# A bound on the indices of every gather in a relational graph network on one core

## What is computed

```
for l in range(n_layers):                       # 3 layers
    xr  = jnp.einsum('nd,rde->rne', x, W_rel[l])   # 8 types
    msg = xr[edge_type, src]
    agg = jax.ops.segment_sum(msg, dst, num_segments=x.shape[0])
    x   = jax.nn.relu(agg + x @ W_root[l] + bias[l])
```

## Time and profile before

| what | value |
|---|---|
| three runs, median | 5964.4 us |
| three runs, lowest and highest | 5960.87 and 5973.35 us |
| the profiled execution: its span, from first to last instruction | 5964.9 us |
| gathers on POOL | 4633, 947 ns each, 4389.2 us |
| matmuls with the gathered rows (L421) | 18792, 2700.1 us |
| matmuls with the relation matrices (L492) | 5568, 1273.8 us |
| bytes moved | 674.77 MB, mean 113 GB/s |

### The profile page before, as it was taken

The page is one execution under the profiler, slowest core; times in us unless marked ns, Lnnn a source line. Parts: engine busy times, 40 slices in busy tenths (PEclk is TensorE's granted clock), DMA queues, the critical chain, the costliest instruction groups (busy, mean ns, idle before and its releaser), DMA issues.

```text
span 5964.9 us, 107654 instructions
## 1 busy us (share of the span) xinstructions
PE 4310.7 (72%) x26040; PEld 3901.4 (65%) x26041; DVE 1844.7 (31%) x3589; ACT 619.0 (10%) x848; POOL 4396.5 (74%) x4659
## 2 busy tenths in 40 slices
PE   4777777777777767777777777766776777776776
PEld 3666666666676656666666666666676666666666
DVE  5222222222222222222222222223333334333333
ACT  3001010010101000000000001000101011101111
POOL 5777777777777677777777777767777777777774
PEclk8898989898989888889999999888888888888887
DMA  6333333333333333333333333333333333333332
GB/s 196 113 111 113 112 112 112 111 114 111 113 112 112 107 111 110 111 111 111 110 111 111 111 110 112 110 106 113 114 113 115 113 113 114 114 113 114 113 113 74
DMA packets 296167, 674.77 MB, mean 113 GB/s; under 512 B 86202, under 2 KB 147387, under 8 KB 295772
## 3 DMA queue, kind: packets, MB, share of 16 engines
q0 software_dynamic: 222384, 607.55, 35.2%
q1 hardware_dynamic: 44686, 37.38, 2.1%
q10 hardware_dynamic: 28702, 26.46, 1.3%
HBM read 645.38 MB, written 25.68 MB: 112 GB/s over the span
## 4 chain that ended last, share of the span: by engine, by line
PE 27%; POOL 25%; issue 20%; SPq 15%; DMA 6%; DVEq 3%; DVE 3%; ACT 1%; ACTq 0%
POOL rows L403 25%; PE bank L421 15%; SPq L352 13%; PE bank L492 10%; DMA rows<-node_table,idx 5%; SPq L347 3%; DVE agg L1003 1%; ACT agg L708 1%; DVEq L986 1%; DVEq L989 1%; PE bank L618 1%; DVEq L1093 1%; PE bank L611 0%; DVE onehot L908 0%; PE bank L537 0%
## 5 line engine op out<-in xcount | busy, mean ns | idle before, releaser
L403 POOL DMA_INDIRECT rows<-node_table,idx x4633 | 4389.2, 947 | 1504.1 <-issue 1316.2
L421 PE MATMUL bank<-onehot,rows 128*128 128x128 f32 x18792 | 2700.1, 305 | 1422.5 <-DVE agg L1003 705.8
L421 PEld LDWEIGHTS bank<-onehot,rows 128*128 128x128 f32 x18792 | 2564.0, 218 | 1571.8 <-issue 1553.2
L1003 DVE TENSOR_TENSOR agg<-bank,agg 128x256 f32 x1566 | 663.7, 424 | 2079.8 <-PE bank L421 1575.6
L492 PE MATMUL bank<-wrel,agg 128*128 128x256 f32 x5568 | 1273.8, 388 | 44.4 <-DVE agg L1016 34.2
L492 PEld LDWEIGHTS bank<-wrel,agg 128*128 128x128 f32 x5568 | 1073.4, 195 | 200.0 <-issue 53.9
L908 DVE TENSOR_TENSOR onehot<-bank,key 128x1152 f32<-128x1152 f32 x525 | 707.0, 1347 | 0.0
L708 ACT COPY agg<-zero_col 128x2304 f32 x174 | 367.2, 2111 | 2928.9 <-PE bank L492 2928.9
L1025 DVE SCALAR_TENSOR_TENSOR acc<-bank,in_first,acc 128x256 f32 x174 | 84.2, 484 | 1777.6 <-PE bank L492 1680.9
L611 PE MATMUL bank<-wroot,nextT 128*128 128x256 f32 x392 | 146.7, 510 | 0.0
L715 ACT COPY acc<-bank 128x256 f32 (+1 forms) x98 | 36.5, 372 | 1004.7 <-PE bank L611 1004.7
(11 more groups left out here) (138 smaller groups left out, 800.1 us busy)
## 6 DMA issues: line engine op xcount, KB each, us to landing
far_rows<-node_table SPq DMA_DIRECT2D x7168, 1.0 KB
rows<-node_table,idx POOLq DMA_INDIRECT x4633
node_table<-new_x ACTq DMA_DIRECT2D x98, 128.0 KB
x_tile<-node_table SPq DMA_DIRECT2D x58, 128.0 KB, 2.2
x_in<-in_x_dram SPq DMA_DIRECT2D x8, 768.0 KB, 11.2
wrel<-in_L_gnn_W_rel_dram SPq DMA_DIRECT2D x6, 1024.0 KB, 8.2
xres<-in_x_dram ACTq DMA_DIRECT2D x48, 128.0 KB
out_dram<-res ACTq DMA_DIRECT2D x48, 128.0 KB
```

The source lines that it names most:

```text
L403: pool.indirect_dma_start(rows[:, s:s + D], None, tables[layer % 2], bass.IndirectOffsetOnAxis(ap=idx[:, g * TPG + k, j:j + 1], axis=0),). ...
L421: last = nc.tensor.matmul(to[:, h, :], of[:, s:s + P], hot[:, hot_k * CH + j, :], start=(j == 0), stop=(j == CH - 1))
L1003: nc.vector.tensor_tensor(window, seg[k % 3].rearrange("p h (r w) -> p h r w", r=R), window, ALU.add).then_inc(agg_added, 1)
```

## The change

Every gather of L403 is given a bound, NP_ - 1 = 6271, the last row of the table, and `oob_is_err=False`: an index above the bound would be skipped silently, its row not written. Before, no bound was given, and `oob_is_err` was at its default, true. The arguments apart, the kernel's text is the same, and the gathers, their order, their sources and destinations, their semaphores and the number of them are the same.

In the program that is built the bound is not part of the instruction but stands in a register. Each gather names a register, and ahead of each of the 4633 gathers POOL's stream has one instruction more that moves the number 6271 into it. Where a gather carried a wait for `seg_ready` (or for `stored`), that wait is now on the move ahead of it, and the gather has none.

```
                             pool.indirect_dma_start(
                                 rows[:, s:s + D], None, tables[layer % 2],
-                                bass.IndirectOffsetOnAxis(ap=idx[:, g * TPG + k, j:j + 1], axis=0),
+                                bass.IndirectOffsetOnAxis(ap=idx[:, g * TPG + k, j:j + 1], axis=0), bounds_check=NP_ - 1, oob_is_err=False,
                             ).then_inc(gathered[k], 16)
```

## The result

The changed kernel took 6193.1 us (median of 4 runs, 6191.28 to 6198.0), the kernel before 5968.9 us in the same comparison. The ratio is 1.0378, with a 95% interval of 1.0363 to 1.0392: 224 us slower. The forecast of no change, 5965 us, was wrong; the range of 5940 to 6480 us and the larger chance of slower held.

A forecast was written before the change was run, and what follows sets the result against it. POOL's gather cadence was taken to bound the kernel: 5964.9 us before, + 0 for the move, under 1.1 for the wait, 0 for the check, gave 5965 us; the 8-in-10 range was 5940 to 6480 us.

The forecast's parts named there:

- What bounds the kernel: POOL's gathers, one every 1.25 us, set the time; anything added to one gather is paid 4633 times.
- The three true stops: POOL's real waits before gathers: one of 6.4 us at the start and two layer changes of 51.8 us together.
- The register move: One move ahead of each gather in POOL's stream, hidden by the sequencer's run-ahead: 0, at most 162 us.
- The sign that I named: In POOL's queue, 4633 MOVE of about 35 ns inside the gathers' bodies would show that the step held.
- The wait on the move: PE's wait, shifted to the move ahead of the gather, costs only at three stops: under 1.1 us, taken as 0.
- The check of 128 indices: Inside each gather, comparing its indices with the bound: taken as 0, between ends of -507 and +990 us.
- The comparison per row: Rival: a new step per row in the gather's body, 107 ns a gather, 6460 us for one step; chance 0.22.
- The small fixed price: Rival: reading the bound or choosing a branch once per gather, 14 to 162 us, 6034 us at 15 ns; chance 0.17.
- The move that is not hidden: Rival: the gap between gathers grows from 305 by 35 ns, bodies unchanged, 6127 us; chance 0.13.
- the cheaper silent mode: Rival: no out-of-range reporting at each gather's end saves, say, 10 ns a gather, 46 us, giving 5919 us; chance 0.13.
- the bound is ignored: Rival: the descriptor code doesn't use the bound, 5965 us, within the forecast; no separate chance given.
- The tail: From the end of POOL's last gather to the execution's end: 56.1 us in the sum of the kernel before.

The follow-up runs named there:

- e9: The changed kernel itself, no edit, timed beside the kernel before and the one-move kernel: 6206.0 us, ratio 1.0385 to the kernel before.
- e10: The changed kernel with its bound register loaded once ahead of all gathers and the waits back on the gathers: 6207.1 us, ratio 1.0381 to the kernel before.
- e3: The changed kernel with oob_is_err=True, an index over the bound being an error: 8459.1 us, ratio 0.9968 to the kernel before, which took about 8480 us there.
- e7: The kernel before with gathers of 64 rows in place of 128, no bound: 8553 us in one execution, median gather body 903 ns.
- e8: Gathers of 64 rows as in e7, with a bound in a register loaded once: 8491 us in one execution, median gather body 942 ns.
- e4: The kernel with one move for all gathers, its bound lowered to 3124 so about half the rows are skipped: body 998 ns, no time given.

## Why the prediction was right and wrong, step by step

*What bounds the kernel* was right. POOL's cadence sets the time, a nanosecond a gather is 4.6 us, and the sum over POOL (bodies, gaps, head, tail) closes in the changed kernel too. The three true stops leave out a fourth, 35.3 us for the first table, which lies inside the 50.8 us of the head, so the sum stands.

*The register move* was priced right, at 0 (e9 against e10), and for the right reason: POOL's sequencer works ahead under gathers too, by about twelve of them. The sign that I named was the wrong one: most moves lie not inside the bodies but just behind a gather's end, and they are those of later gathers. They took 29 ns, not 35. At the start of layer 0, 19 of them had run when 8 gathers had started.

*The wait on the move* was taken at under 1.1 us, with a move and a decode at each of three stops. It cost 0.52 us at each, about 1.6 us, which the times can't show. Where a wait had to be sat out, the gather started 0.78 us after the release with the wait on the move, and 0.26 us after it with the wait on the gather. With POOL starved it is more, as forecast: e3, with the wait on the move, has 591 stops, by the estimate above up to 307 us.

*The check of 128 indices* is the step that failed: "I take 0", from the argument that a loop must compare with some bound anyway. It is 52 ns, and 4633 x 52 = 241 us, the 245 of the bodies. The argument stood on no row, and it was put over the nearest row. The ends that I kept, -507 and +990 us, held it. That the range of 5940 to 6480 us held too is owed to its width and not to a price: its upper end came from a CAST, whose slope the gathers don't follow.

*The rivals.* The comparison per row had the right place and sign (body longer, gap the same). Its 107 ns, from the slope of a CAST, 0.835 ns an element, are twice the whole price and four times the 26 ns of it that go by rows by the straight line. By the same line a row of the gather itself costs 0.67 ns, so the 7.4 ns a row that I read from 947 / 128, my support for a loop of nine steps, was mostly a fixed cost of 860 ns spread over rows; what POOL does in that time, which I took for the making of descriptors row by row, no run opens. The small fixed price had its share too, 26 ns. By this estimate the two rivals together make what happened. That neither does alone is what e7 and e8 show, with 39 ns at 64 rows. The move that is not hidden fell, at e10 and by the moves that run ahead; the cheaper silent mode fell against no bound, though it is cheaper than the error mode. That the bound is ignored fell at e4.

*The tail* was taken as constant. It gave 17.7 us back, since a slower POOL lets PE come closer. PE's waits for rows, which were to grow by nearly what POOL gains in length, grew by 368.8 us (507.3 to 876.1) for POOL's 224.7, while its waits for DVE shrank.

## What to carry to other kernels

Where one engine issues at a fixed cadence and all else follows, an option of its instruction that lengthens it is paid times its count: here 52 ns x 4633 = 241 us, of which the tail gave 17.7 back. Leave a bound out where the indices are known to be in range; nothing in the trace of before shows its price, so a single gather in each form, timed first, settles it. A constant moved to a register each time was free beside these gathers (6206.0 us with 4633 moves, 6207.1 with one), as long as the wait that goes with it was met; the option that reads it, at 52 ns a gather, was not.

## What the runs showed of the hardware

- A gather's body is mostly fixed: 946 ns for 128 rows and 903 for 64, by a straight line 860 ns and 0.67 ns a row. The gap behind it has a median of 304 or 305 ns in every trace, whatever the bound, the mode, the moves or the rows.
- A bound adds 52 ns to the body with a silent skip and 66 with an error, though no index is over it.
- Rows that are skipped cost POOL as much as rows that are fetched (998 ns), and their packets stay in the queue's count (222384), with half of the bytes (304.36 MB for 607.55).
- POOL's sequencer runs register moves about twelve gathers ahead (12 more moves than gathers, at 4421 of 4633 starts). A wait that isn't met costs 0.52 us more on such a move than on the gather (0.78 and 0.26 us from release to start).
- The same kernel took 5970 us or 8480 us, the medians of POOL's bodies and gaps being the same to the nanosecond. Where it took 8480 us, the granted clock was 0.77 in place of 0.88, SP's single rows took 0.75 us in place of 0.51, and the kernel with one move, 3.8% slower otherwise, came out 2% faster. A verdict that is carried by one engine's cadence holds only while that engine sets the pace.
